# Attention of a two-layer kernel: the turned probabilities are copied ahead of the next exponentials, and the mask comes from two 64-row products

## The reference, cut to what matters

```python
local = causal & (j >= i - 64 + 1)
mask = local | g_row & causal | g_col & causal          # g: index 0, 1, 2 or 3
att = jnp.einsum('bhqd,bhkd->bhqk', q, k) / sqrt(16)
att = jnp.where(mask, att, finfo.min)
y = jnp.einsum('bhqk,bhkd->bhqd', softmax(att, -1), v)
```

## Time and profile before

| | us |
|---|---|
| median of 3 runs | 2917.41 |
| lowest, highest | 2910.4, 2920.63 |
| span of the profiled execution | 2907.3 |

### The profile page before, as it was taken

How to read it: one execution, slowest core, us unless ns; L and a number is a source line. 1 busy time by engine, 2 the same in 40 slices (tenths; PEclk the granted TensorE clock), 3 DMA queues, 4 the chain that set the end, 5 groups by cost and what they waited for, 6 DMA issues and landing times.

```text
span 2907.3 us, 90874 instructions
## 1 busy us (share of the span) xinstructions
PE 2504.0 (86%) x33817; PEld 1526.8 (53%) x33817; DVE 1676.1 (58%) x3983; ACT 1620.7 (56%) x4061; POOL 904.5 (31%) x1029
## 2 busy tenths in 40 slices
PE   6999993788787778768999999999999999998998
PEld 4544442555555555533664664655646646546456
DVE  2888873655565556534654655646545545556365
ACT  2887883656565556534644735636536347356354
POOL 0222222545455555541231321321312213213223
PEclk8999996999899999978999999999999999999999
DMA  5555558133313332111111111011011110110110
GB/s 159 147 162 161 161 162 148 27 85 86 69 43 86 71 63 63 42 45 44 44 39 41 25 59 43 17 45 44 16 45 44 60 36 10 59 44 17 45 44 16
DMA packets 386711, 190.06 MB, mean 65 GB/s; under 512 B 271664, under 2 KB 371632, under 8 KB 386224
## 3 DMA queue, kind: packets, MB, share of 16 engines
q1 hardware_dynamic: 386256, 184.01, 24.5%
HBM read 90.10 MB, written 71.30 MB: 56 GB/s over the span
## 4 chain that ended last, share of the span: by engine, by line
PE 55%; issue 16%; DVE 12%; ACT 10%; POOL 5%; DMA 1%; SPq 1%; DVEq 0%; ACTq 0%; POOLq 0%
PE psum L958 9%; PE psum L711 5%; PE psum L799 3%; PE psum L1039 3%; DVE arena L1614 3%; PE psum L1073 3%; PE psum L1062 3%; PE psum L794 3%; PE psum L997 2%; ACT arena L1407 2%; PE psum L787 2%; PE psum L778 2%; ACT arena L1245 2%; PE psum L1091 2%; PE psum L1005 2%
## 5 line engine op out<-in xcount | busy, mean ns | idle before, releaser
L1245 ACT ACTIVATE arena<-psum,scan_sb 64x128 f32<-64x128 f32 x1152 | 310.4, 361 | 139.6 <-PE psum L868 82.0
L1549 POOL TENSOR_TENSOR arena<-arena 128x400 f32<-128x400 f32 x256 | 218.7, 854 | 472.3 <-DVE arena L1942 472.3
L1407 ACT ACTIVATE arena<-psum,arena 128x100 f32<-128x100 f32 x1024 | 268.0, 346 | 127.5 <-DVE arena L1934 127.5
L1934 DVE TENSOR_REDUCE arena<-psum 128x4 f32<-128x400 f32 x256 | 147.1, 575 | 179.3 <-PE psum L1062 177.8
L1467 POOL TENSOR_TENSOR arena<-arena 128x512 f32<-128x512 f32 x132 | 139.8, 1059 | 353.9 <-ACT arena L1263 350.0
L1614 DVE SCALAR_TENSOR_TENSOR arena<-psum,taps_sb,arena 128x511 f32<-128x511 f32 (+2 forms) x288 | 213.6, 747 | 60.7 <-ACT arena L1154 53.9
L711 PE MATMUL psum<-arena,w_in_sb 128*128 128x512 f32 x512 | 229.9, 598 | 0.9 <-issue 0.9
L1681 DVE TENSOR_TENSOR arena<-psum,scan_sb 64x512 f32<-64x512 f32 x290 | 185.9, 673 | 37.8 <-PE psum L886 24.8
L1073 PE MATMUL psum<-ident,arena 128*100 128x128 f32 x1024 | 163.0, 282 | 46.0 <-ACT arena L1413 46.0
L951 PE MATMUL psum<-mask_sb,identb 128*128 128x400 bf16 x960 | 198.9, 342 | 0.0
L778 PE MATMUL psum<-mask_sb,identb 128*128 128x400 bf16 x608 | 163.1, 357 | 35.6 <-issue 32.8
(11 more groups left out here) (219 smaller groups left out, 5036.8 us busy)
## 6 DMA issues: line engine op xcount, KB each, us to landing
arena<-arena SPq DMA_DIRECT2D x144, 128.0 KB
arena<-x SPq DMA_DIRECT2D x32, 512.0 KB, 4.1
arena<-o_d SPq DMA_DIRECT2D x18, 512.0 KB, 5.9
arena<-gate_d SPq DMA_DIRECT2D x18, 512.0 KB, 6.7
v_rows_d<-arena SPq DMA_DIRECT2D x64, 136.0 KB
k_rows_d<-arena SPq DMA_DIRECT2D x64, 136.0 KB
arena<-k_rows_d SPq DMA_DIRECT2D x128, 68.0 KB, 2.1
arena<-v_rows_d SPq DMA_DIRECT2D x128, 68.0 KB, 2.2
```

The costliest lines, as they stand in the source:

```text
L1245: ins = act.activation(dst.rearrange("p (t x a) -> p t x a", x=PP, a=INNER)[upper, :, x], src.rearrange("p (t a) -> p t a", a=INNER)[upper ...
L1407: act.activation(c_soft[s][:, f % 2, u], sc, ACT.Exp, bias=c_max[s][:, u:u + 1]).then_inc(c_act.mark(f"exp{s}{f}u{u}"), 1)
L1549: pool.tensor_tensor(soft, soft, c_rec[s].unsqueeze(2).broadcast_to([P, 4, KEYS]), ALU.mult).then_inc(c_pool.mark(f"prob{s}{f}"), 1)
```

## The change

It has four parts. The first moves ScalarE's copy of step t-3 ahead of the exponentials of step t, in `att_act()` and in ScalarE's list. The second replaces the identity of the mask products by a constant `four_heads` (bf16, 128x128), and each product takes 64 rows of it and of the mask: rows 0 to 63 for the first bank, 64 to 127 for the second. In each half only 32 rows of `four_heads` are not zero, with ones where row and column agree modulo 32; so mask row q is given to all four heads. The third is a wait of TensorE at t = 32 for VectorE's output `y12`. The fourth is the DMA of the constant, 32 KB, and the counts that go with it.

```diff
@@ att_act()
             for t in range(len(ATT) + YE_LAG + 1):
+                if 0 <= t - T_LAG < len(ATT):
+                    names.append(f"pt{ATT[t - T_LAG][1]}{ATT[t - T_LAG][0]}")
                 if t < len(ATT):
                     names += [f"exp{ATT[t][1]}{ATT[t][0]}u{u}" for u in range(QUADS)]
-                if 0 <= t - T_LAG < len(ATT):
-                    names.append(f"pt{ATT[t - T_LAG][1]}{ATT[t - T_LAG][0]}")
@@ SyncE
                 (mask_sb[:], mask_c),
+                (four_heads[:], four_c),
                 (scan_sb[:], scan_c),
@@ TensorE (and the same count on VectorE)
-            pe.wait_ge(weights_loaded, 16 * 23)
+            pe.wait_ge(weights_loaded, 16 * 24)
@@ TensorE, attention
                         for top in range(2):
-
-                            pe.matmul(B(s, top)[:, 0:KT * KEYS], identb[:], mask_sb[:, min(f, 3)], start=True, stop=False,
+                            rows = slice(64 * top, 64 * top + 64)
+                            pe.matmul(B(s, top)[:, 0:KT * KEYS], four_heads[rows], mask_sb[rows, min(f, 3)], start=True, stop=False,
                                       skip_group_check=True)
...
+                    if t == len(ATT):
+                        pe.wait_ge(c_dve.sem, c_dve.at(i, "y12"))
                     stay_warm(f"t{t - T_LAG}", bank[Y_BANKS[2]])
@@ ScalarE, attention
                 for t in range(len(ATT) + YE_LAG + 1):
+                    if 0 <= t - T_LAG < len(ATT):
+                        f, s = ATT[t - T_LAG]
+                        act.wait_ge(c_pe.sem, c_pe.at(i, f"t{s}{f}"))
+                        if f > 0:
+                            act.wait_ge(c_pe.sem, c_pe.at(i, f"pv{s}{f - 1}"))
+                        act.activation(c_pt[s][0:KEYS], bank[TURNED][0:KEYS], ACT.Copy).then_inc(c_act.mark(f"pt{s}{f}"), 1)
                     if t < len(ATT):
...
-                    if 0 <= t - T_LAG < len(ATT):
-                        f, s = ATT[t - T_LAG]
-                        act.wait_ge(c_pe.sem, c_pe.at(i, f"t{s}{f}"))
-                        if f > 0:
-                            act.wait_ge(c_pe.sem, c_pe.at(i, f"pv{s}{f - 1}"))
-                        act.activation(c_pt[s][0:KEYS], bank[TURNED][0:KEYS], ACT.Copy).then_inc(c_act.mark(f"pt{s}{f}"), 1)
@@ constants
+    four = ((part[:, None] % (2 * QF) < QF) & (part[:, None] % QF == part[None, :] % QF)).astype(mybir.dt.np(BF16))
```

More of the change, by code:

```diff
@@ L74, in adaln_two_layers @@
 def adaln_two_layers(nc, x, w_in, taps, w_out, ln_g, ln_b, w_in_init, w_out_init, u1, v1, b1, u2, v2, b2,
-                     cond, wmod, w_attn, w_proj, w_r, w_k, w_v, mu, ident_c, blocks_c, parity_c, mask_c, scan_c, out):
+                     cond, wmod, w_attn, w_proj, w_r, w_k, w_v, mu, ident_c, blocks_c, parity_c, mask_c, four_c, scan_c, out):
     ctx = ExitStack()
@@ L116, in adaln_two_layers @@
         mask_sb = sb("mask_sb", [P, 4, KT * KEYS], BF16)
+        four_heads = sb("four_heads", [P, P], BF16)
         state0 = sb("state0", [P, 2, P])
@@ L1573, in _ @@
                 dve.tensor_scalar(cols, cols, 1.0, None, ALU.add).then_inc(su_dve.mark(f"plus{j + 1}"), 1)
-            dve.wait_ge(weights_loaded, 16 * 23)
+            dve.wait_ge(weights_loaded, 16 * 24)
             own_tap = taps_sb[:].rearrange("p k (c j) -> p k c j", j=TAPS)[:, :, :, TAPS - 1]
@@ L2033 @@
         "mu": np.stack([a("L1_ffn_mu_r").reshape(KT, P).T, a("L1_ffn_mu_k").reshape(KT, P).T], axis=1),
-        "ident_c": ident, "blocks_c": blocks, "parity_c": parity, "mask_c": mask, "scan_c": scan_c,
+        "ident_c": ident, "blocks_c": blocks, "parity_c": parity, "mask_c": mask, "four_c": four, "scan_c": scan_c,
     }
```

## The result

The changed kernel takes 2807.24 us (median of 4 runs, 2804.1 to 2816.39) against 2917.26 for the kernel before beside it: ratio 0.9634, 95% interval 0.9615 to 0.9653, 110 us less. Forecast were 2823 and a range of 2804 to 2868. The profiled execution is the slowest of the four runs (2816.39, span 2814.6). A run's time is thus 1.8 us above its own span; of the 10.1 us between median and span before, most is that the profiled execution was a fast one. The forecast doesn't hang on it, since it takes the same 94 us from both.

What follows compares the result with a forecast made beforehand. A loop of waits over two steps, 4.17 us, was taken to bound the attention's middle. Savings of 9.9 (middle), 0.8 (start) and 1.1 (end) make 11.8 per iteration, 94 over eight: 2917.4 to 2823 us, range 2804 to 2868.

Steps and rivals of the forecast that it cites:

- The loop over two steps: Middle of the attention before: copy, transposes, values, masks, scores, maxima, exponentials, copy takes 4.17 us and covers two steps.
- With the copy first TensorE's own work is the bound: Middle steps: every TensorE wait is covered, so a step takes 1.85 us instead of 2.07, 1.65 with the new masks.
- Legs of the layout: Middle step: predicted times of transposes, copy and exponentials after the masks' start, first 0.90, 1.66, 2.16 with old masks.
- the signs that were named: New profile: masks 1.65 apart, scores' loads 0.1 behind masks, end copies 1.42 apart, copy 0.5 before exponentials, ScalarE awaiting transposes.
- The mask gain of 0.20: From masks to scores on TensorE: 64-row masks save 0.20 us per step, expected 0.15 to 0.25, bounds nothing and 0.25.
- The middle: Steps 6 to 31: 25 steps of 1.65 plus 0.7 for stalls at even heads' outputs, saving 9.9 of 51.83 us.
- The start: Steps 0 to 5 of the attention: four savings of 0.2 us, 0.8 less per iteration.
- The end: Last masks to start of last copy: 5.73 us instead of 6.82, 1.1 less per iteration.
- 1: Rival: masks give nothing, the hole before the scores stays; steps of 1.85, 52 us less, 2865; chance 0.15.
- 2: Rival: the order gives nothing, the masks do; ScalarE stays in a loop; some 26 us less, 2891; chance 0.08.
- 3: Rival: slower, loop through exponentials behind the copy decides from 4.17 us on, predicted 3.06; 2959; chance 0.04 with all slower ways.
- 4: Rival: more than forecast, mask gain 0.25 and no stalls at even heads' outputs; 112 us less, 2805; chance 0.05.

Runs made afterwards that it cites:

- a fill of TensorE's: Changed kernel plus one unread 400-column bf16 product before the transposes in each of steps 6 to 31: 2839.56 us, ratio 0.972 to the kernel before.
- the order alone: Changed kernel with the old 128-row identity masks, the copy still ahead of the exponentials: 2856.36 us, ratio 0.9818 to the kernel before.

## Why the prediction was right, and where its sizes were off

- *The loop over two steps bounds the kernel before.* Shown: cutting it gives 1.85 in every step; leaving it halves a saving and halves an added cost. This part of the prediction was right in mechanism and size.
- *With the copy first TensorE's own work is the bound.* Shown by steps of 1.72 with a fill of TensorE's. Legs of the layout against the profile (transposes, copy, exponentials behind the masks): 0.70, 1.46, 1.96 by the sum, 0.64, 1.40, 1.89 measured; each is 0.06 or 0.07 early, by the larger mask gain. Of the signs that were named one is faint: ScalarE waits for the transposes twice in the 25 steps, because it is nearly full itself (39.19 of 40.32 us).
- *The mask gain of 0.20.* This is the term that was mis-sized: it is 0.26, above its own upper bound of 0.25. The bound let the scores flow at 0.11; they flow at 0.10, and their weights begin to load in the very moment in which the masks begin. In the middle that is 25 x 0.06 = 1.5 an iteration, 12 of the 14.6 us between the forecast gain of 94.2 and the 108.8 of the attentions.
- *The middle.* Forecast 41.95, measured 40.3. The stall at the outputs was put at 0.24 and is 0.02 + 0.20.
- *The start.* Forecast 0.8 less, measured 0.93 (11.68 to 10.75). One thing was missed: with masks and scores of one tiling, step 1 also follows step 0 without a change of tiling and its masks come 0.54 after those of step 0, not 0.90; the wait for the first exponentials takes 0.09 of that back. The steps that the prediction read as 2.3 and 3.3 us are 2.36 and 3.16 in the trace of before; no term of the sum hangs on them.
- *The end.* Forecast 1.1 less, measured 1.16, copies 1.42 apart as before.
- *The new wait and the new DMA cost nothing.* No wait on VectorE stands at t = 32 in the profile (the transposes there wait for the copy). The DMA of the constant stands on SyncE's queue at 21.41 for 0.44 us, and the first batch is still asked for at 43.09, before at 43.60; so the profiles show no cost.
- The rivals: 1, with masks that give nothing, is excluded by the steps of 1.85 with the order alone against 1.59 with both; 2 by the run of the order alone; 3 had 1.1 us of distance, and 2.98 of 3.18 is what the loop through the exponentials takes now; 4 is what came, 2807 where it said 2805, by the mask gain and with the stalls in place. So the time fell outside the 2810 to 2845 that the forecast gave itself, into a case that had a chance of 0.05; the changed kernel's second measurement, 2814.62, lies inside. Which side of 2810 it comes to is within the spread of the runs, but 108.8 against 94.2 us in the attentions is not.

## What to carry to other kernels

Where one engine's waits come in every second step of a software pipeline, follow the loop back by hand and count the steps it spans: here a saving and a cost that stood in every step counted once in two, and an instruction that stands in such a loop only by the order of its list can be moved. Give neighbouring products on TensorE the same tiling, even at the price of zero rows: 0.17 us per change went that way here. And when a bound moves, look at what was put there for the old one: once TensorE was the bound, the fills at the start cost 21 us (what they cost in the kernel before no run shows), while those that still stand in a gap kept the clock.

## What the runs showed of the hardware that was not expected

- A bf16 weight load takes 98 ns with 128 rows, 92 with 64 and 91 with 32, and a float32 load for the same row groups starts in the same hundredth of a microsecond (2003.92 in the timeline).
- The start of the first attention varied by 23 us (1402 to 1425) between profiles with nearly the same code in front. Between the two profiles of the changed kernel it makes 9.4 of the 12.0 us of difference in span, between the two without the fills at the start all 8.0. The cause stays open.
- The granted clock fell to 0.50 for 6.8 us in which TensorE was busy for 6.26, at 7 of 16 ends of an attention and not at the others, though TensorE had been busy for 5.4 of the 6.4 us before in either case; with 6.15 of 6.4 it did not fall.
